# Second attention: units divided by their sums inside the stage by way of memory; token tiles of the routing made by VectorE; first-stage weight kept in memory

## The chip, the cores and the metric

The kernel runs as one launch on one core of a Trainium2 chip. The metric is the device time of one execution in microseconds (us); lower is better. TensorE (PE) multiplies, VectorE (DVE), ScalarE (ACT) and GpSimd (POOL) work on tiles, SyncE (SP) issues most of the transfers. Each engine runs its own list of instructions in order; semaphores order them against each other.

## What is computed

Input `x` is 2 x 2048 tokens of 256 values. The block `x = x + s * g` is applied twice, with `s` an attention and `g` a gate of the normalised `x`:

```python
# first block
s = linear_attention(xn, W_qkv, W_out)          # elu feature maps, numerator / max(denominator, 1e-6)
g = silu(block_forward(xn, ...))                # causal softmax attention, 16 heads of 16,
                                                # then top-2 of 8 experts with a capacity
x = x + s * g
# second block
q, k, v = (x_n @ W).reshape(B, N, H, 2 * hd).transpose(0, 2, 1, 3)   # for Wq, Wk, Wv; 16 heads of 32
scores = (q_r @ k_r.T + q_i @ k_i.T) / sqrt(hd); causal
out = softmax(scores) @ v                       # reshaped to B, N, 512
s = out @ Wo
g = silu(x_n @ int4_quantised(kernel) + bias + (x_n @ a) @ b)
x = x + s * g
```

## The kernel before

The stages run one after the other, each a function: constants and `prepare` to about 100 us, `project_first` to 396, `narrow_attention` to 1242, `after_attention` to 1305, the gate's logits to 1360, `route_and_linear` to 1465, the experts to 1940, `combine_and_project` to 2230, `wide_attention` (the second attention) to 3300, `finish` to the end.

**wide_attention.** Its work is 8 groups of 4 heads, each group cut into 4 blocks of 512 queries: 32 units (g, u). A unit's score tiles are made twice. The "S" form (PE L936) is reduced to row maxima by DVE (L893, L899), L906 and L909 fold the maxima, PE turns them (L973) and SP copies them into a row of the queries' tile (`at_qT<-at_strip`, L805). The "ST" form, keys by queries (PE L944), then goes through the exponential on ACT (L873) into `at_probs`, is multiplied by `v` into `at_acc` (PE L999), and is folded over heads and tiles by POOL (L835), whose result PE multiplies by ones into `at_sum` (L1010). There are 1280 ST steps, 1280 S items, 208 additions on POOL and 112 sum products. `wide_schedule()` simulates the engines and writes one list `body` that all engines follow; it has a unit's two evictions by ACT in it, `otile` (the unnormalised output, L849) and `stile` (the sums, L854). SP stores each three STs later (L788, L791). The units stand in the order 0, 1, 2, 3 in the first group, 2, 0, 3, 1 in the groups 1 to 6 and 3, 2, 1, 0 in the last. When the last unit of a group has been evicted, SP loads the operands of the group after next: six loads of 512 KB (L761) and `v`, 1 MB (L765), 4 MB in all. The score slots are three for ST and three for S, so PE can run at most three items ahead of ACT or DVE. Each engine's order is fixed; nothing overtakes.

**finish.** It multiplies the 512 x 4096 attention output by `Wo`, in 8 blocks of 512 tokens: 32 products of 128x256 a block (L2800), then DVE forms `g * s` (L2783) and adds `x` (L2786), and ACT's queue stores it. Ahead of the products, the class `Attended` loads all sums (`fi_sums`), inverts them on DVE (L1815), stores the inverses, loads them back with each row repeated for the 32 rows of its head (`fi_r`, L1787, 1 MB a block), loads the output (`fi_a`, L1780, 1 MB a block) and multiplies both on POOL (L1820), one instruction a block.

**route_and_linear.** DVE computes for each of the 64 slots a row and a column. POOL makes 64 tiles `rl_tokens` (L2091), DVE four batches `rl_lines` of 16 (L2212), PE multiplies lines by tokens (L2278, in four portions woven into the linear attention's steps), DVE takes the list of token rows from the result (L2223, L2224), and POOL gathers the experts' input rows with 16 indirect transfers (L2013). Beside it run the 32 steps of the linear attention (`normalise` on DVE: L2136, L2140, L2145; PE L2239, L2249, L2261).

**prepare** makes the effective weight `w_ffn` of the last gate (128 x 512 values), which stays on the core until `combine_and_project` uses it (L2727).

## Time and profile before

| | |
|---|---|
| median of 3 runs | 3401.36 us (3400.51 to 3407.37) |
| profiled execution | 3406.8 us, its span 3404.7 us |
| mean granted TensorE clock | 0.928 |
| busy share: PE, DVE, ACT, POOL | 87%, 62%, 46%, 32% |

A share of busy time is a mean over ten stages with different limits, so the stages are read apart. In the tables below a row of a time line has the start in us from the start of the span, the length in us, engine, line, operation, output<-input and, in brackets, how long the engine had been idle before it and what ended that. A row that ends in x4 or the like stands for so many instructions in a run.

### The profile page before, as it was taken

What the parts mean: (1) busy time and instruction counts of PE and PEld (TensorE: products, weight loads), DVE (VectorE), ACT (ScalarE), POOL (GpSimd) and SP (SyncE); (2) the same over time, 40 slices, a digit from 0 to 9 for tenths busy, and PEclk for the clock granted to TensorE, in tenths of its full rate; (3) what the DMA queues carried; (4) which work ended last, traced back from release to release, by engine and by line L of the source; (5) the groups of instructions that cost most, each with busy time, mean ns of one, the idle gap of its engine ahead of it and who ended that gap; (6) DMA issues with size and microseconds to landing.
All of it is one profiled execution on the core that took longest, in us unless ns stands there. A gap on an engine that the chain in (4) does not pass through costs nothing. (4 is left out here: it accounts for less than half of the span.)

```text
span 3404.7 us, 49843 instructions
## 1 busy us (share of the span) xinstructions
PE 2955.3 (87%) x17989; PEld 1375.4 (40%) x17989; DVE 2096.6 (62%) x4626; ACT 1578.7 (46%) x2657; POOL 1088.1 (32%) x561
## 2 busy tenths in 40 slices
PE   4777589999999967789999768859999999999967
PEld 2444333333333326656666434423333333333316
DVE  4778589899999924500000055548878778778615
ACT  1434246667776742122232144415565665665650
POOL 1223200000000001612120122105777777777764
PEclk9899779999999976889999889969999999999989
DMA  4111401111222044323121144450202202211028
GB/s 145 50 49 49 97 22 38 27 29 45 42 45 45 8 79 93 121 56 75 59 89 43 58 137 148 152 137 11 54 11 60 57 15 56 60 28 40 8 55 218
DMA packets 166074, 222.22 MB, mean 65 GB/s; under 512 B 29057, under 2 KB 122833, under 8 KB 163185
## 3 DMA queue, kind: packets, MB, share of 16 engines
q1 hardware_dynamic: 148864, 184.88, 20.8%
q0 software_dynamic: 8704, 25.18, 2.8%
q10 hardware_dynamic: 8304, 9.51, 1.4%
q8 instruction: 123, 2.02, 0.3%
q14 instruction: 79, 0.64, 0.1%
HBM read 138.51 MB, written 80.48 MB: 64 GB/s over the span
## 5 line engine op out<-in xcount | busy, mean ns | idle before, releaser
L835 POOL TENSOR_TENSOR at_probs<-at_probs 128x2048 f32<-128x2048 f32 (+3 forms) x208 | 734.0, 3530 | 330.3 <-ACT at_probs L873 224.6
L873 ACT ACTIVATE at_probs<-at_st 128x512 f32<-128x512 f32 (+3 forms) x1280 | 591.8, 542 | 444.2 <-PE at_st L944 252.3
L372 DVE TENSOR_REDUCE at_part<-at_s 128x1 f32<-128x512 f32 (+3 forms) x1280 | 689.1, 602 | 86.1 <-PE at_s L410 46.2
L354 ACT ACTIVATE at_probs<-at_st 128x1024 f32<-128x1024 f32 (+3 forms) x640 | 541.6, 894 | 293.6 <-PE at_st L437 148.8
L899 DVE TENSOR_REDUCE at_part<-at_s 128x1 f32<-128x512 f32 x768 | 498.8, 684 | 130.7 <-PE at_s L936 127.0
L936 PE MATMUL at_s<-at_kT,at_qT 96*128 96x512 f16 (+3 forms) x1280 | 387.1, 359 | 28.3 <-DMA at_kT<-klo 17.4
L944 PE MATMUL at_st<-at_qT,at_kT 98*128 98x512 f16 (+3 forms) x1280 | 373.4, 354 | 30.6 <-DMA at_qT<-at_strip 20.9
L410 PE MATMUL at_s<-at_kT,at_qT 48*128 48x512 f16 (+3 forms) x1280 | 360.0, 368 | 32.2 <-DMA at_qT<-qhi 12.7
L490 PE MATMUL at_acc<-at_probs,at_v 128*32 128x512 f32 (+3 forms) x2560 | 307.1, 554 | 8.9 <-ACT at_otile L341 8.8
L893 DVE CUSTOM_DVE_ANT_0 at_s<-at_s,at_later 128x384 f32<-128x384 f32 (+3 forms) x512 | 247.5, 498 | 93.5 <-PE at_s L936 92.6
L1820 POOL TENSOR_TENSOR aa_a<-aa_a,aa_r 128x1024 f32<-128x1024 f32 x8 | 18.8, 2346 | 887.1 <-DMA aa_r<-inverse 887.1
L2413 DVE TENSOR_TENSOR ex_ot<-ex_bank,lin_b 128x512 f32<-128x512 f32 x32 | 22.1, 691 | 448.9 <-PE ex_bank L2443 448.9
L429 PE MATMUL at_st<-at_qT,at_kT 50*128 50x512 f16 (+3 forms) x1280 | 284.2, 359 | 15.8 <-DMA at_qT<-at_strip 12.1
L999 PE MATMUL at_acc<-at_probs,at_v 128*32 128x512 f32 (+3 forms) x2560 | 288.8, 539 | 9.7 <-ACT at_otile L849 9.5
L410 PEld LDWEIGHTS at_s<-at_kT,at_qT 48*128 48x128 f16 x1280 | 100.0, 94 | 377.0 <-DVE at_part L372 323.2
L936 PEld LDWEIGHTS at_s<-at_kT,at_qT 96*128 96x128 f16 x1280 | 109.2, 98 | 353.2 <-DVE at_part L899 159.1
L2443 PE MATMUL ex_bank<-lin_w,ex_hT 128*128 128x256 f32 x1024 | 224.5, 380 | 7.0 <-ACT ex_hT L2395 7.0
L2434 PE MATMUL ex_bank<-ex_xT,lin_w 128*128 128x512 f32 x512 | 223.7, 595 | 1.6 <-ACT ex_xT L2387 1.6
L2443 PEld LDWEIGHTS ex_bank<-lin_w,ex_hT 128*128 128x128 f32 x1024 | 193.9, 190 | 43.0 <-ACT ex_hT L2395 13.6
L944 PEld LDWEIGHTS at_st<-at_qT,at_kT 98*128 98x128 f16 x1280 | 122.4, 98 | 195.0 <-ACT at_probs L873 102.0
L2395 ACT ACTIVATE ex_hT<-ex_bank,ex_b 128x512 f32<-128x512 f32 x128 | 87.5, 687 | 232.5 <-PE ex_bank L2434 220.1
L2714 PE MATMUL p_bank<-p_xT,p_w 128*128 128x512 f32 x256 | 129.3, 669 | 28.8 <-ACT p_xT L2576 28.8
(303 smaller groups left out, 3602.0 us busy)
## 6 DMA issues: line engine op xcount, KB each, us to landing
at_v<-v SPq DMA_DIRECT2D x16, 1024.0 KB, 16.8
att<-at_otile SPq DMA_DIRECT2D x64, 256.0 KB, 2.4
lin_w<-in_W SPq DMA_DIRECT2D x16, 1024.0 KB, 8.3
v<-pr_vt SPq DMA_DIRECT2D x32, 256.0 KB, 3.1
exp_out<-ex_ot POOLq DMA_DIRECT2D x32, 256.0 KB, 2.6
v<-p_vt SPq DMA_DIRECT2D x32, 256.0 KB, 4.8
fi_a<-att SPq DMA_DIRECT2D x32, 256.0 KB, 15.6
fi_r<-inverse SPq DMA_DIRECT2D x32, 256.0 KB, 15.6
```

The costliest lines, as they stand in the source:

```text
L354: act.activation(probs[:, quad % RING, heads_down * p:heads_down * (p + 1), off:QB], st_ps[n % st_slots][:, :, off:QB], ACT.Exp, scale=EXP ...
L372: dve.tensor_reduce(part[:, w % 2, qt * HG + h, j:j + 1], s_ps[n % S_SLOTS][:, 0:width], AX.X, ALU.max).then_inc(item_free, 1)
L410: mm = pe.matmul(place[:, 0:width], QT[g % 2][rows, h // heads_down, q0:q0 + P], KT[g % 2][rows, h // heads_down, j * QB:j * QB + width], ...
L429: mm = pe.matmul(place[:, y, off:QB], KT[g % 2][rows, h // heads_down, kc * P:(kc + 1) * P], QT[g % 2][rows, h // heads_down, u * QB + off ...
L490: mm = pe.matmul(acc_ps[32 * h:32 * h + 32, off:QB], V[g % 2][:, kc, 32 * h:32 * h + 32], probs[:, quads % RING, h, off:QB], start=kc == 0 ...
L835: pool.tensor_tensor(total, total, probs[:, slots.slot[quad], :, off:QB], ALU.add).then_inc(add_done, 1)
L873: act.activation(probs[:, slots.slot[quad], h, off:QB], st_ps[n % ST_SLOTS][:, off:QB], ACT.Exp, scale=EXP_SCALE).then_inc(exp_done, 1)
L899: dve.tensor_reduce(part[:, w % 2, qt * HG + h, j:j + 1], s_ps[n % S_SLOTS][:, 0:width], AX.X, ALU.max).then_inc(item_free, 1)
L936: pe.matmul(place[:, 0:width], QT[g % 2][0:K, h, q0:q0 + P], KT[g % 2][0:K, h, j * QB:j * QB + width], start=True, stop=True).then_inc(ite ...
L944: mm = pe.matmul(place[:, off:QB], KT[g % 2][0:K + 2, h, kc * P:(kc + 1) * P], QT[g % 2][0:K + 2, h, u * QB + off:(u + 1) * QB], start=Tru ...
L999: mm = pe.matmul(acc_ps[32 * h:32 * h + 32, off:QB], V[g % 2][:, kc, 32 * h:32 * h + 32], probs[:, slots.slot[quads], h, off:QB], start=kc ...
L2443: mm = pe.matmul(d[:, t * D:(t + 1) * D], hT[cb][:, n, (2 * m + t) * P:(2 * m + t + 1) * P], w2[k][:, n, :], start=n == 0, stop=n == NFF - 1)
```

## The change

- **wide_attention**: for 31 of the 32 units, six hops are added at fixed distances, counted in ST steps after the unit's second eviction (`HOPS`). SP stores the four rows of sums (keep, 3 steps), loads them back as a column tile of 128 x 16 (turn, 8), DVE inverts the column (invert, 13), SP stores it (return, 15) and loads it with each head's row spread over 32 partitions into the one tile `share` (spread, 20, four transfers), POOL multiplies `otile` by `share` (scale, 27), and SP stores the output (store, 30). `otile` and `column` are double, `stile` and `share` single: spread waits for the scale of the unit before, the eviction of `stile` for the keep of the unit before. For the last unit DVE inverts the whole `stile` and multiplies. The list `body` is the same.
- **finish**: no sums, no inverses, no `fi_r`, nothing on POOL. Each block of the output is one load of 1 MB into one of four tiles; the first stands ahead of the weights' load. Blocks 4 to 7 wait for the products of the block four before.
- **route_and_linear**: the 64 token tiles are made by DVE, 16 after each batch of lines; PE's portions stand one step earlier; one `normalise` instead of two stands ahead of the wait for PE.
- **prepare, combine_and_project**: `w_ffn` is stored to memory by SP at the end of `prepare` (256 KB) and loaded again behind the projection's weights, all of which PE and DVE wait for; `mean`, `rstd`, `stats` live in a narrower context.

```diff
+HOPS = {"keep": 3, "turn": 8, "invert": 13, "return": 15, "spread": 20, "scale": 27, "store": 30}
+def after_units(body, per_unit, hops, last):
+    seen, due, n = {}, [], 0
+    for ev in body:
+        if ev[0] == "ST":
+            n += 1
+        elif ev[0] == "EV":
+            seen[ev[1]] = seen.get(ev[1], 0) + 1
+            if seen[ev[1]] == per_unit and ev[1] != last:
+                due += [(n + wait, len(seen), kind, ev[1]) for kind, wait in hops.items()]
+    return sorted(due)
...
-        otile = c.sb("otile", [P, QB], F32)
+        otile = c.sb("otile", [P, 2, QB], F32)
         stile = c.sb("stile", [P, QB], F32)
+        column = c.sb("column", [P, 2, QB // 32], F32)
+        share = c.sb("share", [P, QB], F32)
...
+                if kind == "keep":
+                    sp.wait_ge(sum_ready, t + 1)
+                    sp.dma_start(sums[t], stile[0:P:32, :]).then_inc(sum_kept[t % 2], 16)
+                elif kind == "turn":
+                    sp.wait_ge(sum_kept[t % 2], 16 * (t // 2) + 16)
+                    sp.dma_start(column[:, t % 2, :], sums[t].rearrange("h (c n) -> (h c) n", c=32)
+                                 ).then_inc(column_ld[t % 2], 16)
+                elif kind == "return":
+                    sp.wait_ge(inverted, t + 1)
+                    sp.dma_start(inverse[t].rearrange("h (c n) -> (h c) n", c=32), column[:, t % 2, :]
+                                 ).then_inc(inverse_kept[t % 2], 16)
+                elif kind == "spread":
+                    sp.wait_ge(inverse_kept[t % 2], 16 * (t // 2) + 16)
+                    if t:
+                        sp.wait_ge(scaled, t)
+                    for h in range(HG):
+                        sp.dma_start(share[32 * h:32 * h + 32, :], inverse[t][h:h + 1, :].to_broadcast([32, QB])
+                                     ).then_inc(share_ld, 16)
+                elif kind == "store":
+                    sp.wait_ge(scaled, t + 1)
...
+            def scale(unit):
+                t = place_of[unit]
+                pool.wait_ge(out_ready, t + 1)
+                pool.wait_ge(share_ld, 16 * HG * (t + 1))
+                pool.tensor_tensor(otile[:, t % 2, :], otile[:, t % 2, :], share[:, :], ALU.mult).then_inc(scaled, 1)
...
+                    if t:
+                        act.wait_ge(sum_kept[(t - 1) % 2], 16 * ((t - 1) // 2) + 16)
                     act.activation(stile[:, :], sum_ps[:, :], ACT.Copy).then_inc(sum_ready, 1)
...
+            def invert(unit):
+                t = place_of[unit]
+                dve.wait_ge(column_ld[t % 2], 16 * (t // 2) + 16)
+                dve.reciprocal(column[:, t % 2, :], column[:, t % 2, :]).then_inc(inverted, 1)
...
+            dve.reciprocal(stile[:, :], stile[:, :]).then_inc(whole_inverted, 1)
...
+            dve.tensor_tensor(otile[:, 1, :], otile[:, 1, :], stile[:, :], ALU.mult).then_inc(whole_scaled, 1)
...
-                pool.tensor_scalar(tokens[:, n, :], count[:, 0:WIDE], column[:, n:n + 1],
-                                   token[:, n % NT:n % NT + 1], ALU.is_equal, ALU.mult).then_inc(tokens_ready, 1)
...
+                for m in range(n, n + CHUNK):
+                    ts(tokens[:, m, :], count[:, 0:WIDE], column[:, m:m + 1], token[:, m % NT:m % NT + 1],
+                       ALU.is_equal, ALU.mult).then_inc(slots_ready, 1)
                 normalise()
...
+            sp.wait_ge(w_kept, 16)
+            sp.dma_start(w_ffn[:, :, :], w_saved).then_inc(w_ld, 16)
...
-            dve.wait_ge(w_ld, 64)
+            dve.wait_ge(w_ld, 80)
...
+            sp.dma_start(a[0][:, :, :], rows[0, :, :, 0:QB]).then_inc(ld[0], 16)
             sp.dma_start(w[:, :, :], W["Wo"].rearrange("(g p) n -> p g n", p=P)).then_inc(w_ld, 16)
-
-            attended.load(sp)
-
-        @block.gpsimd
-        def _(pool):
-            attended.divide(pool)
+            for blk in range(1, NB):
+                b, k = blk // (NB // B), blk % (NB // B)
+                if b:
+                    pe_s.wait(sp, "x3", blk - NB // B)
+                sp.dma_start(a[k][:, :, :], rows[b, :, :, k * QB:(k + 1) * QB]).then_inc(ld[k], 16)
```

Three places of the second attention show how the hops stand in the engines' orders. The first is SP's order at the end of group 1, where the operands of group 3 are loaded (`att` is the output in memory, `sums` and `inverse` the hops' memory). Before:

```order
L761 DMA at_kT<-klo 32x4x2048
L765 DMA at_v<-v 128x2048
L788 DMA att<-at_otile 128x512
L791 DMA sums<-at_stile 4x512
L805 DMA at_qT<-at_strip 2x512 x4
```

The changed kernel there:

```order
L812 DMA sums<-at_stile 4x512
L815 DMA at_column<-sums 128x16
L819 DMA inverse<-at_column 128x16
L826 DMA at_share<-inverse 32x512 x4
L785 DMA at_qT<-qhi 32x4x2048
...
L785 DMA at_kT<-klo 32x4x2048
L789 DMA at_v<-v 128x2048
L830 DMA att<-at_otile 128x512
L812 DMA sums<-at_stile 4x512
L815 DMA at_column<-sums 128x16
L819 DMA inverse<-at_column 128x16
L826 DMA at_share<-inverse 32x512 x4
```

The four hops of unit (1, 3) now stand ahead of the loads, and the sums of unit (1, 1) are stored, as before, behind them, but now three further transfers follow, each of which waits for the one before.

The second is DVE's order where it inverts unit (1, 1) (L955 and L961 are the changed kernel's lines for L893 and L899, the row maxima). Before:

```order
L893 ISA at_s,at_part<-at_s,at_later 128x384
L893 ISA at_part 128x1
L899 TENSOR_REDUCE at_part<-at_s 128x1 x3
L893 ISA at_s,at_part<-at_s,at_later 128x512
L893 ISA at_part 128x1
```

The changed kernel there:

```order
L955 ISA at_s,at_part<-at_s,at_later 128x384
L955 ISA at_part 128x1
L961 TENSOR_REDUCE at_part<-at_s 128x1 x3
L943 RECIPROCAL at_column<-at_column 128x16
L955 ISA at_s,at_part<-at_s,at_later 128x512
L955 ISA at_part 128x1
```

The reciprocal, with its wait for the column, stands between two row maxima. The third is POOL's order in group 2 (L885 is the changed kernel's line for L835). Before:

```order
L835 TENSOR_TENSOR at_probs<-at_probs 128x4x384
L835 TENSOR_TENSOR at_probs<-at_probs 128x4x256
L835 TENSOR_TENSOR at_probs<-at_probs 128x4x128
L835 TENSOR_TENSOR at_probs<-at_probs 128x2048 x7
L835 TENSOR_TENSOR at_probs<-at_probs 128x4x384
```

The changed kernel there:

```order
L885 TENSOR_TENSOR at_probs<-at_probs 128x4x384
L885 TENSOR_TENSOR at_probs<-at_probs 128x4x256
L885 TENSOR_TENSOR at_probs<-at_probs 128x4x128
L885 TENSOR_TENSOR at_probs<-at_probs 128x2048 x6
L868 TENSOR_TENSOR at_otile<-at_otile,at_share 128x512 x2
L885 TENSOR_TENSOR at_probs<-at_probs 128x2048
L885 TENSOR_TENSOR at_probs<-at_probs 128x4x384
```

The scales of the units (2, 2) and (2, 0) stand in a row between the sixth and the seventh whole addition.

## Rows read from the trace of the kernel before

**Rows 1.** Windows of the second attention: length, busy time by engine, clock, DMA share, GB/s

```profile
2400.00:2600.00 200.00, 194.87 (x1340) 66.49 (x1333) 162.98 (x405) 121.82 (x265) 147.07 (x42) 1.00 0.22 51
```

**Rows 2.** Time line of SP's queue at the end of group 1

```profile
2560.49 0.43 SPq L788 DMA_DIRECT2D att<-at_otile  x1
2569.15 0.52 SPq L791 DMA_DIRECT2D sums<-at_stile  x1
```

**Rows 3.** DMA view, 2560 to 2584: issues, KB, us from issue to landing

```profile
at_v<-v SPq DMA_DIRECT2D x1, 1024.0 KB, 18.3
att<-at_otile SPq DMA_DIRECT2D x1, 256.0 KB, 18.5
```

**Rows 4.** Time line of DVE behind those loads

```profile
2576.79 0.69 DVE L893 CUSTOM_DVE_ANT_0 at_s<-at_s,at_later 128x512 f32<-128x512 f32 x1
```

**Rows 5.** Time line of POOL and PE in group 2

```profile
2646.41 4.55 POOL L835 TENSOR_TENSOR at_probs<-at_probs 128x2048 f32<-128x2048 f32 x1 [0.80 <-ACT at_probs L873]
...
2651.59 1.06 PE L1010 MATMUL at_sum<-at_probs,all_ones 128*32 128x512 f32 x8
```

**Rows 6.** Groups by shape: busy us, mean ns of one, idle us before

```profile
L835 POOL TENSOR_TENSOR at_probs<-at_probs 128x512 f32<-128x512 f32 x32 | 40.7, 1272 | 2.5
```

**Rows 7.** Lines L906 and L909 of DVE: ns of one, least, median, most

```profile
L906 DVE TENSOR_REDUCE at_rowmax<-at_part x32: 179/195/222, 2244.9 to 3239.1; 128x16 f32<-128x16 f32 x8, 128x16 f32<-128x32 f32 x8, 128x16 f32<-128x48 f32 x8, 128x16 f32<-128x64 f32 x8
...
L909 DVE SCALAR_TENSOR_TENSOR at_shift<-at_rowmax,at_nothing x32: 178/898/4287, 2245.1 to 3239.4; 128x16 f16<-128x16 f32 x32
```

**Rows 8.** Time line of PE in combine_and_project

```profile
2007.37 17.05 PE L2714 MATMUL p_bank<-p_xT,p_w 128*128 128x512 f32 x32 [3.63 <-ACT p_xT L2576]
...
2201.00 15.70 PE L2714 MATMUL p_bank<-p_xT,p_w 128*128 128x512 f32 x32 [3.53 <-ACT p_xT L2576]
2216.53 7.03 PE L2720 MATMUL p_bank<-p_w,p_xT 128*128 128x512 f32 x16
```

**Rows 9.** Time line of the start of finish, all engines

```profile
3298.06 0.49 SPq L791 DMA_DIRECT2D sums<-at_stile  x1
...
3305.12 3.35 DVE L1815 RECIPROCAL fi_sums<-fi_sums 128x512 f32<-128x512 f32 x1 [62.06 <-DMA fi_sums<-sums]
...
3324.58 8.68 PE L2800 MATMUL fi_bank<-fi_w,fi_a 128*128 128x256 f32 x32 [27.20 <-POOL fi_a L1820]
```

**Rows 10.** Time line and window of the later blocks of finish

```profile
3330.01 4.51 POOL L1820 TENSOR_TENSOR fi_a<-fi_a,fi_r 128x2048 f32<-128x2048 f32 x1 [5.56 <-DMA fi_r<-inverse]
...
3339.74 4.51 POOL L1820 TENSOR_TENSOR fi_a<-fi_a,fi_r 128x2048 f32<-128x2048 f32 x1 [5.22 <-DMA fi_r<-inverse]
...
3392.80 7.17 PE L2800 MATMUL fi_bank<-fi_w,fi_a 128*128 128x256 f32 x32 [2.27 <-POOL fi_a L1820]
...
3400.68 0.42 DVE L2786 TENSOR_TENSOR fi_o<-fi_o,all_x_all 128x256 f32<-128x256 f32 x1
```

**Rows 11.** Window of finish, columns as in rows 1

```profile
3330.00:3340.00 10.00, 8.61 (x41) 7.26 (x40) 7.88 (x10) 0.00 (x0) 4.77 (x2) 1.00 1.06 215
```

**Rows 12.** DMA view of finish: issues with us to landing

```profile
inverse<-fi_sums SPq DMA_DIRECT2D x1, 256.0 KB, 2.1
```

**Rows 13.** Time line of route_and_linear

```profile
1386.04 42.96 POOL L2091 TENSOR_SCALAR rl_tokens<-rl_count,rl_column,rl_token 128x64 f16<-128x64 f32 x64 [78.80 <-DVEq L2208]
...
1430.75 1.30 POOL L2013 DMA_INDIRECT lin_xin<-z_rows,lin_rows_at  x1 [1.75 <-DVE lin_rows_at L2224]
```

**Rows 14.** Time line of DVE in route_and_linear

```profile
1385.68 0.20 DVE L2207 TENSOR_SCALAR rl_column<-rl_column 128x64 f32<-128x64 f32 x1
...
1386.28 2.37 DVE L2212 TENSOR_TENSOR rl_lines<-rl_count,rl_line 128x2048 f16<-128x2048 f32 x1
...
1389.79 2.37 DVE L2212 TENSOR_TENSOR rl_lines<-rl_count,rl_line 128x2048 f16<-128x2048 f32 x1
```

**Rows 15.** Time line of PE at the end of route_and_linear

```profile
1455.71 6.03 PE L2261 MATMUL rl_out<-rl_w_out,rl_nT 128*128 128x256 f32 x16
1465.03 0.34 PE L2422 MATMUL ex_bank<-all_identf,lin_b1n 64*128 64x64 f32 x1 [3.29 <-PEq L40]
```

More of the change, by code:

```diff
@@ L780, in _, with hop @@
             load(sp, 1)
-            n_stored, ended = [0, 0], []
-            def store(unit, k):
+            count, waiting = 0, list(after)
+            def hop(kind, unit):
                 g, u = unit
-                n_stored[k] += 1
-                if k == 0:
-                    sp.wait_ge(out_ready, n_stored[0])
-                    sp.dma_start(out[g, :, u * QB:(u + 1) * QB], otile[:, :]).then_inc(out_stored, 16)
-                else:
-                    sp.wait_ge(sum_ready, n_stored[1])
-                    sp.dma_start(sums[g, :, u * QB:(u + 1) * QB], stile[0:P:32, :]).then_inc(sum_stored, 16)
@@ L809, in _ @@
                     load(sp, ev[1][0] + 2)
-            while ended:
-                store(*ended.pop(0)[:2])
-            sp.wait_ge(out_stored, 16 * len(units))
-            sp.wait_ge(sum_stored, 16 * len(units))
+            while waiting:
+                hop(*waiting.pop(0)[2:])
+            g, u = units[-1]
+            sp.wait_ge(whole_scaled, 1)
+            sp.dma_start(out[g, :, u * QB:(u + 1) * QB], otile[:, 1, :]).then_inc(out_stored[1], 16)
+            for k in range(2):
+                sp.wait_ge(out_stored[k], 16 * (len(units) // 2))
         @block.gpsimd
@@ L885, in _ @@
             dve.wait_ge(nothing_ready, 1)
+            count, waiting = 0, [x for x in after if x[2] == "invert"]
+            def invert(unit):
+                t = place_of[unit]
+                dve.wait_ge(column_ld[t % 2], 16 * (t // 2) + 16)
+                dve.reciprocal(column[:, t % 2, :], column[:, t % 2, :]).then_inc(inverted, 1)
             for ev in body:
+                count += ev[0] == "ST"
+                while waiting and waiting[0][0] <= count:
+                    invert(waiting.pop(0)[3])
                 if ev[0] == "S":
@@ L2219, in _ @@
             link(tt(gate[:, :, :], gate[:, :, :], keep[:, :, :], ALU.mult))
-            for _ in range(2):
-                normalise()
+            normalise()
             dve.wait_ge(turned, 1)
@@ L2728, in body, with finish @@
                                            xT[:, n, (2 * m + t) * P:(2 * m + t + 1) * P],
-                                           C["w_ffn"][:, n, :], start=n == 0, stop=n == NF - 1)
+                                           w_ffn[:, n, :], start=n == 0, stop=n == NF - 1)
                     pe_s.step(f"y{m}", mm)
             blocks_ahead(pe, body)
-def finish(nc, W, att, sums, inverse, x_all, g_all, out):
+def finish(nc, W, att, x_all, g_all, out):
     jobs = [(f"x{t}", "dve", f"mul{t}") for t in range(4)]
@@ L2745, in finish @@
         banks = Banks(c, jobs, {"dve": dve_s}, ring=4)
-        attended = Attended(c, att, sums, inverse, 32, pe_s, "x3")
+        rows = att.rearrange("(b g) r t -> b r g t", b=B)
         block = c.block()
@@ L2854, in build @@
             combine_and_project(nc, C, W, x, s_out, exp_out, gather_at, gate, x_all, scales(1),
-                                qk[1], v[1], g_all)
-            wide_attention(nc, "at1", C, *qk[1][0], *qk[1][1], groups(v[1]), att[1], sums[1])
-            finish(nc, W, att[1], all_sums[1], inverse[1], x_all, g_all, out)
+                                qk[1], v[1], g_all, w_saved, w_kept)
+            wide_attention(nc, "at1", C, *qk[1][0], *qk[1][1], groups(v[1]), att[1], sums1, inverse1)
+            finish(nc, W, att[1], x_all, g_all, out)
 _NAMES = {"L0_attn_x": "x", "L0_attn_W_qkv": "W_qkv", "L0_attn_W_out": "W_out", "L0_ffn_ln1_g": "ln1_g",
```

107 lines of the change are left out of this document (61 added, 46 removed).

## Prediction

> **What bounds the kernel now.** The windows of the second attention come first, since the change is mostly there: in 200 us PE is busy for 194.87, DVE for 162.98, POOL for 147.07, ACT for 121.82, at a granted clock of 1.00 [rows 1]. PE is the bound and takes its instructions in order, so a wait on any engine costs nothing until PE stands still for it, and then all of it. SP's queue and its transfers' landing times come next [rows 2, 3], because the hops go through them. In finish the time line is read: PE waits for POOL's product, and POOL for its transfers [rows 9, 10]. In the routing the question is who sets the end of POOL's 43 us row of tokens [rows 13].
>
> **Finish.** The last sums leave ACT just ahead of their store at 3298.06 [rows 9]; today PE starts its first block at 3324.58, 26.5 us later, and later blocks are paced by POOL's starts, 3330.01 and 3339.74, 9.73 us apart, of which 4.51 is the product and 5.22 a wait for memory [rows 10]. Afterwards: from 3298.0 DVE's reciprocal of the whole tile takes 3.35 [rows 9], the product of 128x512 about 0.7 (as the 128x512 instruction of [rows 4]). Unit (7, 1)'s hops, one after the other on SP, are done only about then too (four landings of 2.1 [rows 12] from 3290.6 on, with reciprocal, issues and scale: 3302.7), so the last store is issued at about 3304 and landed 2.1 later; the stage ends near 3306. The first 1 MB and the weights' 0.5 MB take 1.57 MB / 215 GB/s [rows 11] = 7.3 and some 2 of latency: PE starts at 3315.5. The first block takes 8.68 [rows 9], seven more 7.0 each (7.17 is the length of one with the overlap of its ends [rows 10]), so 3373.2; 1.0 for DVE's last two and 3.6 for the store (last DVE end 3401.10 against the span's 3404.7) give 3377.8. That is **-27**. The transfers, 13.1 MB, need 61 us at 215 GB/s, from 3306 to 3367, so they do not set the end.
>
> **Routing.** POOL's 64 tokens end at 1429.0, the first gather starts at 1430.75 [rows 13]. On DVE a batch of lines with one `normalise` takes 3.51 (1386.28 to 1389.79), and a small scalar operation of 128x64 takes 0.20 [rows 14]: 4 x 3.51 + 64 x 0.20 = 26.8, from 1386.3 to 1413.1; four small ones, one `normalise` and PE's last portion add 3 to 4, so the first gather starts near 1417.4, 13.3 earlier. The linear attention's remaining pairs are the same and waited for PE's turn of the tokens; its end, 1455.71 + 6.03, sets the experts' first product at 1465.03 [rows 15]. I take **-13**; the ends are 0 (DVE's 12.8 us more come back in the pairs) and -23.
>
> **DVE's inversion behind the group loads.** At the end of the groups 0 to 5 4 MB go out in one piece on SP's queue. The `att` store issued right behind them at 2560.49 landed 18.5 us later, `v` ahead of it 18.3 [rows 2, 3]; a 256 KB transfer alone takes 2.1 [rows 12]. So a transfer on that queue waits for what is queued before. The sums of (1, 1) are stored at 2569.15 [rows 2], behind them still. Afterwards the loads also leave about 2 us later: unit (1, 3)'s spread stands ahead of them, four issues of 0.43 [rows 2] and its wait for the inverse. So `att` lands at 2579.0 + 2 = 2581, the sums no earlier, and turn 2.1 later, at 2583.5 with its issue. DVE's place for the reciprocal is just ahead of the maximum at 2576.79 [rows 4]: it waits 6.7. Queued behind it are the row maxima for which PE's three S slots wait; PE has run two or three ahead of DVE already, so it loses about 6.5, and it has nothing else to run. Six places: **+39**. The ends are 0 (the sums' four packets slip past: kept at 2571.3, the turn issued five steps after it near 2573 and landed at 2575.1, ahead of 2576.8) and 43. I take the upper row because the 18.5 is of the same queue and place. One page has a price for the small hops: the Trainium skill, "DMA: Bandwidth & Descriptors", section "Latency and other measured facts", gives some 0.8 us as the least for a tiny transfer by way of memory. The nearest row, 2.1 for 256 KB [rows 12], is no tiny transfer, so the trace does not decide; with 0.8 the turn would land 1.3 sooner and the sum be 8 lower.
>
> **POOL's two scales in a row.** In the groups 2 to 5 the scales of (g, 2) and (g, 0) stand together ahead of the whole addition that now starts at 2646.41 [rows 5]. There is one `share`: the spread of (2, 0) waits for the scale of (2, 2), which ends at 2645.6 + 1.27 = 2646.9 (1272 ns for 128x512 on POOL [rows 6]). Four issues, 1.7, and a landing of 2.1 to 2.4 make 2651.1, the second scale 2652.4, and the addition is 6.0 late. It ends today at 2650.96, PE's sum product follows at 2651.59 [rows 5], a slack of 0.6: PE loses 5.4. Four places: **+22**, between 0 and 24. Elsewhere a scale stands alone, after 7 steps of time for its spread.
>
> **POOL's multiplications themselves** are 31 x 1.27 = 39 us of POOL, of whose 200 us 53 are idle [rows 1]. Nearly all fall into idle time; where an addition follows without a pause, PE feels them: I take **+4**, between 0 and 39.
>
> **TensorE's clock.** It is 1.00, 2.4 GHz, through the second attention [rows 1]. In the projection, after idles of 3.63 and 3.53 us, 32 products took 17.05 and 15.70 where 16 of the same shape take 7.03 at full speed, so 14.06: 3.0 and 1.6 lost beside the idle itself [rows 8]. The change makes ten new idles of 5 to 7 us; at 2 each **+20**, between 8 and 30.
>
> **The rest.** 31 reciprocals of 128x16 on DVE: about 0.2 each by L906, which reads one tile, hidden in DVE's 37 idle us of 200 [rows 1]; L909, two inputs beside POOL, takes up to 4287 ns [rows 7], so the bound is 31 x 4.3, mostly in idle time too. Stores and hops in memory are small beside a DMA share of 0.22 [rows 1]. The weight's store ends prepare later by 0.5 at most; its load ends well ahead of the first product that needs it. **+0.5**.
>
> **The sum**: -27 - 13 + 39 + 22 + 4 + 20 + 0.5 = +45.5. The profiled execution, 3406.8, would become 3452; it lies 5.4 above the median of the runs, so the forecast is 3401.4 + 45.5 = **3447**.
>
> **The rivals.**
> - *Waits half absorbed.* Score steps after each wait run faster than before, since ACT, DVE and POOL have 20 to 40% idle [rows 1]; PE itself has only 5 of 200 us, which speaks against it. 39, 22 and 20 become 19, 11 and 8: +2.5, 3404, no change.
> - *The sums are not held by the loads.* Their four packets use few of the 16 engines. The 18.5 of `att` [rows 3] speaks against it. Without the six waits and their clock (12): -5.5, 3396, still within the bound. The Trainium skill, "DMA: Bandwidth & Descriptors", section "Queues, rings and completion order", says that completion is not first in, first out over an issuing engine, only in each ring; that is this rival's mechanism, and where the rings are evenly loaded it gives my forecast.
> - *All hops hidden* (the other side): inversion and second scale both find their data in time, because the hops take under 1.5 us and `share` is free in time. Then -27 - 13 + 4 + 0.5 = -35.5, **3366**. It decides at DVE's 2576.8: sums turned before that, faster; the issue of `att` and the 4 MB ahead speak against it.
> - *Worse*: the routing gains nothing (DVE is late for its pairs), the waits and the clock are at their upper ends, POOL costs 10: -27 + 0 + 43 + 24 + 10 + 30 = +80, 3481.
>
> **How the numbers follow.** Forecast 0.51 (its own range 3420 to 3472), half absorbed 0.14, sums not held 0.10, all hidden 0.15, worse 0.10. A measurement of this kernel can tell 0.2%, 6.8 us, from no change: 3394.6 to 3408.2. Faster: all hidden, and 0.05 of "not held": 0.20. Same: 0.05 of it and 0.08 of half absorbed: 0.13. Slower: 0.67. The range leaves out most of "all hidden" and the top of "worse": 3385 to 3475.
>
> **What would show it.** Right: POOL absent from finish and PE's blocks 7.0 apart; first gather near 1417; DVE's reciprocal at six places after an idle of 6 to 7 us with the column's transfer as its releaser, and PE idle by as much; two POOL multiplications 5.5 apart before one late addition in groups 2 to 5; windows of the second attention below 1.00 of clock. Wrong: the sums' store landing within 3 us behind the loads, PE busy for 194 of 200 still, and the stage's end at 3306 or earlier.

## The result: slower by 0.8%, and the profile after

| | before | changed |
|---|---|---|
| median of 5 runs | 3401.36 us (3400.46 to 3407.37) | 3431.00 us (3422.85 to 3436.43) |
| ratio | | 1.0079, interval 1.006 to 1.0098 |
| profiled execution, span | 3406.8, 3404.7 | 3426.0, 3424.3 |
| first exponential of the second attention (L873, now L925) | 2276.4 | 2260.0 |
| last exponential of it | 3291.4 | 3341.3 |
| from the first to the last | 1015.0 | 1081.4 |
| from the last to the end of the span | 113.3 | 83.0 |

The kernel became slower by 29.6 us at the median, 19.6 between the two profiled spans: 16.5 gained ahead of the second attention, 66.4 lost in it, 30.3 gained behind it. The forecast of 3447 was 16 too high, with the sign and the places right.

The windows of the second attention, with the columns of [rows 1]:

```profile
2400.00:2600.00 200.00, 186.85 (x1262) 63.24 (x1255) 154.42 (x369) 113.69 (x249) 141.13 (x45) 0.97 0.23 57
2600.00:2800.00 200.00, 181.17 (x1204) 59.77 (x1202) 143.55 (x347) 112.94 (x246) 142.80 (x45) 0.97 0.15 39
```

PE did 1262 and 1204 products in 200 us, where [rows 1] has 1340, and the clock is below 1.00. The two lines that the hops add to DVE and POOL, with what they waited for (ns of one; then us and times of the idles):

```profile
L943 DVE RECIPROCAL at_column<-at_column x31: 239/244/254, 2292.1 to 3343.8; 128x16 f32<-128x16 f32 x31
...
  DMA at_column<-sums: 73.9, 9
```

```profile
L868 POOL TENSOR_TENSOR at_otile<-at_otile,at_share x31: 1260/1277/1309, 2303.8 to 3348.8; 128x512 f32<-128x512 f32 x31
...
  DMA at_share<-inverse: 14.6, 4
```

Of DVE's nine idles, three lie behind its last row maximum (4.5, 27.3 and 19.0 us), where nobody waits. The other six, 23.1 us in all, are at the six places behind the group loads: 4.6, 3.3, 4.7, 3.9, 3.3 and 3.3. POOL's four are the second scales of the groups 2 to 5. The second place in full, first SP's queue (compare [rows 2]), then DVE (compare [rows 4]) and PE:

```profile
2547.89 1.72 SPq L826 DMA_DIRECT2D at_share<-inverse  x4
2549.65 0.42 SPq L785 DMA_DIRECT2D at_qT<-qhi  x1
...
2552.72 0.43 SPq L789 DMA_DIRECT2D at_v<-v  x1
2559.50 0.34 SPq L830 DMA_DIRECT2D att<-at_otile  x1
2560.86 0.52 SPq L812 DMA_DIRECT2D sums<-at_stile  x1
2570.29 0.33 SPq L815 DMA_DIRECT2D at_column<-sums  x1
```

```profile
2571.88 0.25 DVE L943 RECIPROCAL at_column<-at_column 128x16 f32<-128x16 f32 x1 [3.30 <-DMA at_column<-sums]
```

```profile
2569.57 0.39 PE L1005 MATMUL at_s<-at_kT,at_qT 96*128 96x512 f16 x1
2572.83 0.39 PE L1005 MATMUL at_s<-at_kT,at_qT 96*128 96x512 f16 x1 [2.87 <-DVE at_part L955]
```

The turn (L815) is issued the moment the 8 KB of sums have landed: 9.4 us after their own issue. The turn lands 1.6 us later, and DVE has stood for 3.30 by then. PE wrote one more S item at 2569.57 and stood for 2.87. The other place, in group 2, on POOL and PE (compare [rows 5]):

```profile
2638.12 4.54 POOL L885 TENSOR_TENSOR at_probs<-at_probs 128x2048 f32<-128x2048 f32 x1 [1.89 <-PE at_acc L1068]
2642.63 1.28 POOL L868 TENSOR_TENSOR at_otile<-at_otile,at_share 128x512 f32<-128x512 f32 x1
2647.72 1.27 POOL L868 TENSOR_TENSOR at_otile<-at_otile,at_share 128x512 f32<-128x512 f32 x1 [3.81 <-DMA at_share<-inverse]
2648.94 7.89 POOL L885 TENSOR_TENSOR at_probs<-at_probs 128x2048 f32<-128x2048 f32 x2
```

```profile
2653.49 1.93 PE L1079 MATMUL at_sum<-at_probs,all_ones 128*32 128x512 f32 x8 [4.78 <-POOL at_probs L885]
```

Behind both idles the clock fell. Behind the one at 2572.83 it is 0.50 from 2574.7 to 2578.1. The windows of the inversion of the first of the six places (group 0, PE idle for 4.07 us until 2438.8) and of this sum product, 7 and 4 us:

```profile
2438.00:2445.00 7.00, 6.16 (x18) 1.32 (x18) 5.08 (x11) 1.41 (x3) 1.61 (x1) 0.51 0.15 41
2653.00:2657.00 4.00, 3.51 (x21) 0.94 (x22) 0.00 (x0) 0.00 (x0) 3.83 (x2) 0.57 0.00 0
```

That is, for most of both windows, the level of 1.2 GHz, and the eight sum products took 1.93 where [rows 5] has 1.06.

The gains. In the routing DVE makes the tokens in four portions; PE's first product of the experts (compare [rows 15]) is 17.6 us earlier:

```profile
1387.37 3.65 DVE L2281 TENSOR_SCALAR rl_tokens<-rl_count,rl_column,rl_token 128x64 f16<-128x64 f32 x16
```

```profile
1420.38 1.30 POOL L2084 DMA_INDIRECT lin_xin<-z_rows,lin_rows_at  x1 [117.53 <-DVE lin_rows_at L2291]
```

```profile
1447.44 0.34 PE L2487 MATMUL ex_bank<-all_identf,lin_b1n 64*128 64x64 f32 x1 [8.04 <-PEq L40]
```

In finish PE runs through its eight blocks without a pause (compare [rows 9, 10]):

```profile
3351.15 0.69 DVE L995 TENSOR_TENSOR at_otile<-at_otile,at_stile 128x512 f32<-128x512 f32 x1
3351.86 0.34 SPq L850 DMA_DIRECT2D att<-at_otile  x1
3354.42 0.38 SPq L2821 DMA_DIRECT2D fi_a<-att  x1
```

```profile
3361.59 57.95 PE L2869 MATMUL fi_bank<-fi_w,fi_a 128*128 128x256 f32 x256 [14.50 <-DMA fi_w<-in_Wo]
```

### The profile page after: what moved, and what is told of

Its sections match the earlier page's. It is cut to its first block and busy times, and to the rows that moved or that the text cites. A ratio compares the mean times of both kernels' runs of the same rounds, so it can differ in the third digit from the quotient of the medians.

```text
span 3424.3 us, 50007 instructions
## 1 busy us (share of the span) xinstructions
PE 2964.7 (87%) x17989; PEld 1372.0 (40%) x17989; DVE 2106.8 (62%) x4722; ACT 1581.0 (46%) x2657; POOL 1046.3 (31%) x520
## 5 line engine op out<-in xcount | busy, mean ns | idle before, releaser
L885 POOL TENSOR_TENSOR at_probs<-at_probs 128x2048 f32<-128x2048 f32 (+3 forms) x208 | 733.0, 3528 | 349.4 <-ACT at_probs L925 242.4
L925 ACT ACTIVATE at_probs<-at_st 128x512 f32<-128x512 f32 (+3 forms) x1280 | 593.1, 541 | 511.6 <-PE at_st L1013 285.6
L961 DVE TENSOR_REDUCE at_part<-at_s 128x1 f32<-128x512 f32 x768 | 498.3, 684 | 142.0 <-PE at_s L1005 138.4
L1005 PE MATMUL at_s<-at_kT,at_qT 96*128 96x512 f16 (+3 forms) x1280 | 394.1, 364 | 53.0 <-DMA at_kT<-klo 19.1
L490 PE MATMUL at_acc<-at_probs,at_v 128*32 128x512 f32 (+3 forms) x2560 | 307.2, 554 | 8.9 <-ACT at_otile L341 8.8
L955 DVE CUSTOM_DVE_ANT_0 at_s<-at_s,at_later 128x384 f32<-128x384 f32 (+3 forms) x512 | 247.2, 497 | 108.4 <-PE at_s L1005 107.7
L1068 PE MATMUL at_acc<-at_probs,at_v 128*32 128x512 f32 (+3 forms) x2560 | 295.8, 550 | 9.7 <-ACT at_otile L902 9.5
L2508 PEld LDWEIGHTS ex_bank<-lin_w,ex_hT 128*128 128x128 f32 x1024 | 193.9, 190 | 43.0 <-ACT ex_hT L2460 13.6
```

Source lines behind the costliest of these rows:

```text
L490: mm = pe.matmul(acc_ps[32 * h:32 * h + 32, off:QB], V[g % 2][:, kc, 32 * h:32 * h + 32], probs[:, quads % RING, h, off:QB], start=kc == 0 ...
L885: pool.tensor_tensor(total, total, probs[:, slots.slot[quad], :, off:QB], ALU.add).then_inc(add_done, 1)
L925: act.activation(probs[:, slots.slot[quad], h, off:QB], st_ps[n % ST_SLOTS][:, off:QB], ACT.Exp, scale=EXP_SCALE).then_inc(exp_done, 1)
L961: dve.tensor_reduce(part[:, w % 2, qt * HG + h, j:j + 1], s_ps[n % S_SLOTS][:, 0:width], AX.X, ALU.max).then_inc(item_free, 1)
L1005: pe.matmul(place[:, 0:width], QT[g % 2][0:K, h, q0:q0 + P], KT[g % 2][0:K, h, j * QB:j * QB + width], start=True, stop=True).then_inc(ite ...
L1068: mm = pe.matmul(acc_ps[32 * h:32 * h + 32, off:QB], V[g % 2][:, kc, 32 * h:32 * h + 32], probs[:, slots.slot[quads], h, off:QB], start=kc ...
```

## The experiments

Each run is the changed kernel with one edit, unless it says otherwise. Each has a ratio to the kernel before, run on the same chip, since the median of the kernel before differs from chip to chip: it was 3397.35 us beside the scales, the loads behind the strip's copy, both edits and ACT's queue, 3405.10 beside the next four, and 3400.87 beside the run without the hops. The expectations were written in absolute times from the changed kernel's 3431, so a gain is compared by the ratios (0.001 is 3.4 us; the changed kernel has 1.0079) or by the length of the attention. "Attention" is the time from its first to its last exponential, 1015.0 before and 1081.4 in the changed kernel. The theory: six waits of DVE and four of POOL on the hops, with the half clock behind them, make the 66 us. The rivals: the hops are slow wherever they stand; or other edits of that stage cost.

### Without the hops

```diff
-HOPS = {"keep": 3, "turn": 8, "invert": 13, "return": 15, "spread": 20, "scale": 27, "store": 30}
+HOPS = {"keep": 3, "store": 3}
...
-                    sp.wait_ge(scaled, t + 1)
+                    sp.wait_ge(out_ready, t + 1)
```

> The changed kernel without the division of 31 units in the second attention (left out: turn, invert, return, spread, scale; the sums and the outputs are stored three steps after the evictions, as before the change; the last unit is still divided), loads where they were. My account (all of the second attention's +66 us comes from waits for the hops, the half clock behind them and 3 to 4 us of POOL's multiplications): the attention is back at 1015 us from its first exponential to its last, no new idles of PE, and the time is 3401 - 16 - 30 = 3355, a ratio of 0.986. Rival (part of the 66 us is from other edits in that stage, such as the double output tile or the late store): the attention stays above 1020 us, time above 3360, with the faster version of the hops (1021 us) no longer near the floor.

3363.32 (3361.22 to 3363.82), ratio 0.9888 (0.987 to 0.9907). The attention takes 1015.6, PE has no new idle. So the whole of its loss hangs on the hops, and the double output tile costs nothing. The rest of the change alone is worth 37.6 us at the median, less than the 46.8 (16.5 and 30.3) that the two profiles differ by ahead of and behind the attention; this run's own profile starts its first exponential at 2262.4 and ends 83.3 behind the last, like the changed kernel's. The expected 3355 and 0.986 were missed by 8 us, outside the interval: the time lies above 3360, as the rival had it, but the attention, which the rival needs above 1020, does not.

### The four second scales

```diff
-                due += [(n + wait, len(seen), kind, ev[1]) for kind, wait in hops.items()]
+                late = 4 if ev[1] in [(g, 0) for g in range(2, 6)] else 0
+                due += [(n + wait + late * (kind in ("scale", "store")), len(seen), kind, ev[1])
+                        for kind, wait in hops.items()]
```

> The changed kernel, but the scale and the store of the units (2,0), (3,0), (4,0) and (5,0) stand four score steps later, so that the whole addition comes ahead of the second scale. Theory (one share tile makes the second of two scales in a row late, and the addition behind it): POOL's four idles of 3.4 to 3.8 us go, and the four steps of 6.0 to 6.8 us, 25 in all: 3431 becomes 3406; the six idles of DVE stay. Rival (PE waited there for something else, such as the sum product's own place, or the scale moves its cost to the next addition): 3424 to 3431.

3405.39 (3397.50 to 3415.64), ratio 1.0026 (1.0012 to 1.004). The attention takes 1056.2, 25.2 less. POOL there:

```profile
2644.46 1.27 POOL L870 TENSOR_TENSOR at_otile<-at_otile,at_share 128x512 f32<-128x512 f32 x1
2645.70 4.53 POOL L887 TENSOR_TENSOR at_probs<-at_probs 128x2048 f32<-128x2048 f32 x1
2650.19 1.28 POOL L870 TENSOR_TENSOR at_otile<-at_otile,at_share 128x512 f32<-128x512 f32 x1
```

The addition goes first, its 4.53 us cover the second spread, and neither scale waits. DVE's six idles are as they were (3.4 to 4.8). In the attention's length the theory's 25 is met. By the ratios the gain is 0.0053, 18 us, with an interval of some 8 us either way that includes 25.

### The loads behind the strip's copy

```diff
-                    load(sp, ev[1][0] + 2)
+                    loads.append((count + LOADS_AFTER, ev[1][0] + 2))
...
+                    if loads and loads[0][0] <= count:
+                        load(sp, loads.pop(0)[1])
```

`LOADS_AFTER` is 25 score steps, and the loads go out behind the next copy of a strip.

> The changed kernel with the 4 MB of group loads issued later by SP: behind the strip's copy that follows the unit's hops, instead of ahead of the sums' store. Queue theory (the sums are held by the 4 MB ahead of them on SP's queue): the six idles of DVE ahead of the reciprocal (3.3 to 4.7 us each) fall under 0.5, the six steps of 5.4 to 7.1 us in the second attention go, 38 us in all, 3431 becomes 3393; four idles of POOL ahead of the second scale (3.4 to 3.8) stay. Rival (the place of the reciprocal is too early for three hops in any case, or the hops are slow for another reason): DVE's six idles stay above 2.5 us and the time is within 8 us of 3431. Second rival: the loads now hold the copy of the next strip, and PE waits for that instead: time between, 3400 to 3425, with idles of PE ended by the strip's transfer.

3440.91 (3433.43 to 3443.70), ratio 1.0125 (1.010 to 1.0151): slower still. DVE's six idles are gone, as the queue theory has it. But the time rose, by a rival that I had not named: the keys come too late. SP, then PE, at the second place:

```profile
2590.24 2.48 SPq L842 DMA_DIRECT2D at_qT<-at_strip  x4
2592.76 0.40 SPq L786 DMA_DIRECT2D at_qT<-qhi  x1
...
2595.22 0.44 SPq L786 DMA_DIRECT2D at_kT<-klo  x1
```

```profile
2610.23 0.61 PE L1008 MATMUL at_s<-at_kT,at_qT 96*128 96x512 f16 x1 [3.44 <-DMA at_kT<-klo]
```

The S items run ahead of the ST steps by more than a unit, so the next group's keys are due near 2606.8, some 50 us after the loads' old place, not a whole group later. PE idles of 3.4 to 6.3, 29.9 us in all, took the place of 2.9 to 4.3, 20.4 in all. The loads have a window: behind the turn, and early enough for their transfers, since the last of the keys, issued at 2595.22, landed 15 us later. With both edits of this and the last section:

> The loads later and the four scales later, together. If the two causes are separate the gains add up: 38 + 25 = 63, 3431 becomes 3368, 1.0% under the kernel before; granted clock 1.00 through the second attention as before. If one wait hides the other or a new one takes their place: 3380 to 3405.

3414.30 (3411.15 to 3418.49), ratio 1.0053 (1.0036 to 1.0071). Attention 1069.0, which is 26.6 under the 1095.6 of the loads alone: the scales' gain adds to this as to the changed kernel, and the wait for keys stays. Neither expected range was met: the loads' later place had been taken for a gain of 38 and was a loss.

### The loads from ACT's queue

```diff
-                elif ev[0] == "EV" and ev[2] == 0 and ev[1] == last_unit[ev[1][0]] and ev[1][0] + 2 < GROUPS:
-                    sp.wait_ge(pv_done, quads_done[ev[1]])
-                    load(sp, ev[1][0] + 2)
...
+                    if unit == last_unit[unit[0]] and unit[0] + 2 < GROUPS:
+                        load(act, unit[0] + 2)
```

> The changed kernel with the group loads issued from ACT's queue, behind the eviction of the group's last output, at the same time as before; the hops stay on SP's queue. Queue theory in its narrow form (only what stands ahead on the same queue holds the sums): DVE's six idles go, minus 38 us, plus 7 issues of 0.45 on ACT at six places, of which PE feels 0 to 3 each: 3393 to 3411. Rival (the 16 engines are simply busy with 4 MB, whatever queue it came by): the sums still land 5 us and more after their issue, DVE idles above 2.5, the time is 3425 to 3445.

3424.39 (3419.58 to 3425.42), ratio 1.0082 (1.0061 to 1.0104). The narrow queue theory falls. The sums, stored on SP's otherwise empty queue, were issued at 2559.77, the turn at 2567.96, so they still took 8.2 us to land, and DVE still idled by 1.9 to 2.5 at all six places. The loads stood 12.5 us ahead of the sums' store (2547.23 to 2559.77) and in the changed kernel 11.2; these 1.3 us are the difference of DVE's waits at this place (2.04 and 3.30). Six idles of PE of only 1.5 to 1.9 us are left there, and behind three of them the clock still fell to 0.50 for 3.4 us. The attention takes 1075.1, 6.3 less, but the ratio is the changed kernel's. So the rival holds in the landing (over 5 us) and in the ratio, and DVE's idles are just under its 2.5. The DMA view of 2558.3 to 2564.3 (queue, kind: packets, MB, share; then the issues) shows the hold; q10 is ACT's queue, SP's q1 does not appear in it at all:

```profile
q10 hardware_dynamic: 331, 1.28, 103.0%
q8 instruction: 1, 0.02, 1.4%
issues: line engine op xcount, KB each, median us to landing
att<-at_otile SPq DMA_DIRECT2D x1, 256.0 KB, 9.9
```

The `att` store was issued at the start of that window from the other queue and not one of its packets moved in 6 us, while the loads' did; q1's first packets come in the next stretch. So here the hold is by what had been handed to the 16 engines before, from ACT's queue as from SP's. It is no rule for every pair of queues: in the changed kernel's routing, from 1425 to 1440, POOL's gathers (q0, 533 packets) and SP's stores (q1, 1360) moved in the same stretch. The Trainium skill, "DMA: Bandwidth & Descriptors", section "Issuing engines are not separate DMA queues", says that a second issuing engine saves only issue time; this run agrees. The same page of the Trainium skill, in the section "Queues, rings and completion order", has an engine alternate between the queues it has work for, packet by packet; by that the store's 2 KB packets would have moved beside the loads', and the window shows none. The measurement decides here. Why the second queue is held is left open.

### Fewer bytes ahead

```diff
-            eng.dma_start(V[g % 2][:, :, :], v[g]).then_inc(v_ld[g % 2], 16)
+            n = NKC if g < 2 else 1
+            eng.dma_start(V[g % 2][:, 0:n, :], v[g][:, 0:n, :]).then_inc(v_ld[g % 2], 16)
```

> The changed kernel with a smaller load ahead of the sums' store: of v of the groups 2 to 7 only the first of 16 key tiles is loaded (the other rows keep older values, so a part of the computation uses wrong v), 3.06 MB instead of 4 at the same place. Bytes theory: the loads are through 4.5 us sooner (0.94 MB at 210 GB/s), the sums land that much sooner, and DVE's six idles of 3.3 to 4.7 us become 0 to 0.5: 38 us less, 3431 becomes about 3393. Rival (the hold is one of landing times of single transfers, not of bytes ahead): idles above 2 us stay.

3417.36 (3408.84 to 3421.32), ratio 1.0028 (1.0012 to 1.0045), attention 1061.9, 19.5 less. DVE's six idles became 2.7, 1.2, 2.5, 1.2, 0.9 and 0.8: 9.3 us instead of 23.1. With 0.94 MB less ahead the sums of the second place land 7.2 us after their issue instead of 9.4. By the ratios the gain is 17 us. The direction is the bytes theory's, but 2.3 us an idle came off and not 4. The step that failed is the price of the bytes: `v`, issued 3.1 and 3.3 us behind the first load, landed 17.9 us after its issue in the changed kernel and 15.2 here, so the loads were through 2.5 sooner and not 4.5. The sums moved with them, by 2.2. The rival, idles of 2 us and more, holds at two of six places, where the idles had been longest.

### The hops after the inversion later

```diff
-HOPS = {"keep": 3, "turn": 8, "invert": 13, "return": 15, "spread": 20, "scale": 27, "store": 30}
+HOPS = {"keep": 3, "turn": 8, "invert": 20, "return": 22, "spread": 25, "scale": 32, "store": 35}
```

> The changed kernel with HOPS invert 20, return 22, spread 25, scale 32, store 35, loads where they were. Position theory: seven steps are about 5 us, more than the idles of 3.3 to 4.7, so DVE's six idles go (38 us). The two scales in a row move by five steps and may meet another addition: if their four steps of 6.4 go too, 3368; if they stay, 3393; rival: the wait only moves to POOL's scale at the six places, because spread follows return by three steps, 3400 to 3431.

3419.93 (3415.39 to 3424.65), ratio 1.0046 (1.0028 to 1.0064). DVE's six idles are gone, and POOL's four old ones too. The rival's new wait is there, though with the unit before: unit (1, 3)'s return now stands behind the loads, and its spread goes out 17.8 us after it. On SP, then on POOL:

```profile
2553.13 0.43 SPq L789 DMA_DIRECT2D at_v<-v  x1
2553.61 0.43 SPq L819 DMA_DIRECT2D inverse<-at_column  x1
2571.43 1.73 SPq L826 DMA_DIRECT2D at_share<-inverse  x4
```

```profile
2574.83 1.27 POOL L868 TENSOR_TENSOR at_otile<-at_otile,at_share 128x512 f32<-128x512 f32 x1 [10.62 <-DMA at_share<-inverse]
```

Five idles of POOL of 9.4 to 10.6 us, each followed by a PE idle of 4.2 to 5.4, and one of 3.7. The attention takes 1059.0, and the time is in the rival's range. A later reciprocal does cure DVE's wait, but a later set of hops runs into the loads with another unit.

### The hops before the loads

```diff
+SOON = {"keep": 3, "turn": 6, "invert": 10, "return": 11, "spread": 14, "scale": 27, "store": 30}
...
+                    if unit == last_unit[g] and g + 2 < GROUPS:
+                        load(sp, g + 2)
```

`SOON` is for the last unit of the groups 0 to 5, the loads stand right behind its spread, and the four scales stand later as above.

> The scales as in the run with the four later scales; and for the last unit of the groups 0 to 5 the hops stand closer (keep 3, turn 6, invert 10, return 11, spread 14 steps after the second eviction), with the group loads right behind the spread, so that no hop stands behind a load and the loads land before the first S item of the next but one group's operands is due (that was the new wait when the loads stood behind the strip's copy: issue at 2592.76, PE waiting for the keys until 2610.2). Theory: DVE's six idles and PE's waits for keys both go: 3405 becomes 3405 - 38 = 3367 (3360 to 3378), about 1% under the kernel before. Rival (the loads need their early place too, or the closer hops are themselves not landed in time): DVE or PE idles of over 2 us at these six places, 3380 to 3410.

3373.82 (3368.37 to 3388.24), ratio 0.9912 (0.9892 to 0.9933): faster than both kernels. SP's queue at the second place:

```profile
2561.43 0.52 SPq L823 DMA_DIRECT2D sums<-at_stile  x1
2563.14 0.34 SPq L826 DMA_DIRECT2D at_column<-sums  x1
2567.17 0.32 SPq L830 DMA_DIRECT2D inverse<-at_column  x1
2568.58 1.71 SPq L837 DMA_DIRECT2D at_share<-inverse  x4
2570.33 0.42 SPq L796 DMA_DIRECT2D at_qT<-qhi  x1
```

The turn follows the sums' store by 1.7 us instead of 9.4. Neither DVE nor POOL nor PE waits for a hop ahead of DVE's last row maximum, and the windows are

```profile
2400.00:2600.00 200.00, 193.52 (x1326) 66.66 (x1324) 165.66 (x404) 122.01 (x270) 151.26 (x48) 1.00 0.24 57
2600.00:2800.00 200.00, 194.19 (x1342) 64.74 (x1341) 160.24 (x389) 124.34 (x270) 154.83 (x48) 1.00 0.16 39
```

The attention takes 1021.2, 35.0 less than with the scales alone; by the ratios the gain is 39 us, and the theory had 38. The six waits and the clock behind them are thus priced by an edit that removes them. That leaves 5.6 us over the run without the hops for the division by way of memory; its ratio, 0.9912 against 0.9888, says the same with some noise.

### The tokens back on POOL

```diff
+            pool.wait_ge(at_ready, 1)
+            for n in range(SLOTS):
+                pool.tensor_scalar(tokens[:, n, :], count[:, 0:WIDE], column[:, n:n + 1],
+                                   token[:, n % NT:n % NT + 1], ALU.is_equal, ALU.mult).then_inc(tokens_ready, 1)
...
-                for m in range(n, n + CHUNK):
-                    ts(tokens[:, m, :], count[:, 0:WIDE], column[:, m:m + 1], token[:, m % NT:m % NT + 1],
-                       ALU.is_equal, ALU.mult).then_inc(slots_ready, 1)
```

> The changed kernel with the 64 token tiles made by POOL again, all else as changed. If the token tiles alone brought the earlier start of the experts (1447.4 instead of 1465.0), the experts start near 1463 again and the time is 15 to 18 above the changed kernel's 3431: 3447. Rival (the gain came from the different places of normalise and of PE's portions): under 5 us above.

3456.34 (3447.64 to 3465.30), ratio 1.0157 (1.0136 to 1.0177), against the changed kernel's 1.0079: 26 us more. The row of tokens on POOL, and the experts' first product:

```profile
1389.80 43.15 POOL L2162 TENSOR_SCALAR rl_tokens<-rl_count,rl_column,rl_token 128x64 f16<-128x64 f32 x64 [81.53 <-DVEq L2279]
```

```profile
1459.68 3.62 PE L2331 MATMUL rl_out<-rl_w_out,rl_nT 128*128 128x256 f32 x8
...
1470.51 0.33 PE L2491 MATMUL ex_bank<-all_identf,lin_b1n 64*128 64x64 f32 x1 [3.29 <-PEq L40]
```

The rival of other edits is out: the experts start 23 us later. That is 5 more than the theory gave; PE was at its slower clock in the last pairs there, where eight products took 3.62 and in the changed kernel 1.89. In the nine profiles with the changed routing the experts start at 1447.3 to 1460.5, median 1450.7, so a single profile holds this stage to some 13 us; the ratio of the runs is the firmer number.

## Why the prediction held, and where its terms were off

| term | predicted | measured in the profiled spans |
|---|---|---|
| finish and the last store | -27 | -30.3 |
| routing | -13 | -17.6 at the experts' start, -16.5 at the attention's |
| inversions behind the loads, idle of PE | +39 | +20.4 |
| second scales, idle of PE | +22 | +18.5 |
| TensorE's clock | +20 | about +24, an estimate |
| POOL's multiplications and the rest | +4.5 | about +5, PE's small idles; not measured apart |
| sum | +45.5 | +19.6 between the spans (these terms give 21); the medians differ by 29.6 |

**Inversions.** The mechanism was right in each part: the sums behind the 4 MB, the turn behind the sums, DVE, the S slots, PE, six places. The step that failed is its size, "it waits 6.7" and "so it loses about 6.5". The loads left at 2549.65, 11.2 us ahead of the sums' store; my 2 us of delay for them had left 10. The sums landed 9.4 after their issue, where mine, landing with `att`, came 11.9 after theirs. The turn took 1.6 and not 2.1: 8 KB, where I took the 256 KB row. DVE waited 3.3 there. Of that PE lost 2.87, nearly all, as I had it. The idles of PE at the six places are 4.1, 2.9, 4.3, 3.5, 2.9 and 2.9, 20.4 in all, where I had 39. The 0.8 us of the Trainium skill ("DMA: Bandwidth & Descriptors", section "Latency and other measured facts") for a tiny transfer, which I set beside the sum, is a least time, and the runs stay well above it: the turns took 1.5 to 2.7, median 1.6, the returns 1.4 at the least and at the median.

**Second scales.** Right in place and number: two scales 5.1 apart (2642.63 to 2647.72), I had 5.5. The four idles of PE are 4.8, 4.65, 4.4 and 4.6, I had 5.4. Each step of the attention there is 6.0 to 6.8, and moving the scale took back 25.2 in all; the 6.7 over the idles are the clock's, as far as the count below tells.

**The clock** was the term I was least sure of. By the clock's records, the second attention spends 54.6 us at 1.2 GHz later than 75 us behind its start, before the change 6.8. Half of the 47.8 more is 24, if PE were busy all that time. PE's idle time in the attention, small idles included, is 44.0 more than before, 38.9 of it in the ten new idles. Together this gives 68, and 66.4 was measured. The same count in the other runs, idle and half clock, against what their attention takes over 1015.0: the later scales, 26.1 + 13.7 against 41.2; ACT's queue 42.7 + 15.4 against 60.1; both edits 35.8 + 22.2 against 54.0; fewer bytes 31.7 + 13.7 against 46.9; later hops 30.6 + 15.4 against 44.0; the later loads 53.7 + 34.1 against 80.7, the worst, 7 off. With the hops before the loads it is 5.6 + 0 against 6.3. So the half clock is somewhat over a third of the price of a wait here. No run keeps the idles and takes the clock away, so this share is an estimate and not shown by itself.

**Routing.** The fourth portion of tokens ended at 1412.0 (predicted 1413.1) and the gather started at 1420.38 (predicted 1417.4): 10.4 earlier and not 13.3, since PE's last portion stood behind other work. What I undersold is behind it: the linear attention's last products ended at 1439.4 instead of 1461.7. The idle of PE of 7.32 us that the kernel before had ahead of 1454.83, beside the gathers, is not in this profile. But it is not gone: with the same routing, the later hops, the hops before the loads and the run with fewer bytes have one of 10.6 us there, and their experts start at 1456.9 to 1460.5, those of the other six at 1447.3 to 1453.0. So part of the 17.6 is luck of the profile; against the median of the nine, 1450.7, the gain is 14.3, and my 13 was nearer than this profile says. What brings that idle is open. The term is read better at the experts' start than at the gather's.

**Finish.** First load issued at 3354.42, 13.1 after the last exponential (I had 14.5), PE at 3361.59, 7.2 later (I had 9.3: the weights landed 6.4 after their issue, faster than the 215 GB/s of a stage with the spread rows in it), eight blocks in 57.95 (57.7).

**The rivals.** "All hops hidden" was, at DVE's 2576.8, the right point to decide by: when the sums are turned in time and the second scale does not wait (the hops before the loads) the kernel is at 3374, where that rival said 3366. "Waits half absorbed" is out: of DVE's 23.1 us at the six places PE lost 20.4. "Worse" is out, since the routing did gain. "The sums are not held by the loads" is out, in the changed kernel and even with the loads on another queue.

**The sum of the medians.** 29.6 of difference against 19.6 in the profiled spans: the profile of before lies 5.4 above its median, that of the changed kernel 5 below. So the sum of the terms was 26 too high and the forecast of the medians only 16; that the second is smaller is luck of the two profiles, and 18.6 of the 26 are the inversions' size. The changed kernel's runs spread over 13.6 us, those of before over 6.9. What makes them spread is not settled; the routing's two lengths are one candidate, and the last section has another.

## What to carry to other kernels

Here a small transfer was only as quick as the bulk load issued before it from SP's or ACT's queue, so a chain of small hops belongs ahead of a bulk load, and the bulk load has a last date as well; both ends should be read from the trace before moving it, because the same 4 MB cost 35 us of the attention in their old place (the scales moved, 1056.2 against 1021.2) and 48 in the later one (1069.0). An instruction that waits for a transfer in the middle of a full engine's order makes that engine's whole order wait, and when TensorE is the bound and stands for 3 to 5 us, as here, the slower clock behind it adds by estimate about 0.6 of that again (24 on 38.9). A single buffer between two consumers that stand in a row turns two short steps into a round trip; putting a long independent instruction between them was worth 25 us of the attention (18 by the ratios) without any memory.

## What the runs showed of the hardware that was not expected

- At the second place the sums' 8 KB took 9.4 us behind 4 MB on the same queue and 8.2 us with the 4 MB on the other queue, 1.7 when nothing was ahead. A separate issuing queue was no way round.
- DVE's small instructions with two inputs from on-chip memory sometimes last as long as POOL's addition beside them. In the run with the later loads, DVE and POOL:

```profile
2390.65 0.63 DVE L974 SCALAR_TENSOR_TENSOR at_shift<-at_rowmax,at_nothing 128x16 f16<-128x16 f32 x1
2391.32 4.44 DVE L978 SCALAR_TENSOR_TENSOR at_shift<-at_rowmax,at_shift 128x16 f16<-128x16 f32 x1
```

```profile
2389.97 1.27 POOL L871 TENSOR_TENSOR at_otile<-at_otile,at_share 128x512 f32<-128x512 f32 x1
2391.21 4.51 POOL L888 TENSOR_TENSOR at_probs<-at_probs 128x2048 f32<-128x2048 f32 x1
```

DVE's started 0.1 us after POOL's and ended with it; PE then stood for 3.24 us, and the attention lost 6.3 at that one place. It happens by alignment: a PE idle of 3.2 us from it is in the profiles of three of the ten kernels with the change (the later loads, both edits and fewer bytes). Before the change the second of the two instructions was never held (178, 179 and 182 ns, least, median and most of 32); in the changed kernel the most is 4462. The reciprocal of the hops, with one input, took 239 to 254 ns in all 31 cases. The Trainium skill, "GPSIMD Engine Reference", section "1. Specifications", says that the two engines share their ways to on-chip memory and names DVE instructions with two inputs there, beside those in a two-port mode, as the ones in contention; the rows agree for two inputs. It may be why the changed kernel's runs spread more; that was not tested.
